# A plain latent attention's first keys and queries in another order, and a down product that waits chunk by chunk

## What the kernel computes

```
q_hk  = (hidden_q @ Wq.T).reshape(b, s, H, K)
q_big = einsum('bshk,hkq->bshq', q_hk, w_kc_q)
kv_rope = kv_c * cos + rotate_half(kv_c) * sin
q_r = einsum('bshq,hqr->bhsr', q_big, W_qr)
k_r = einsum('bld,hdr->bhlr', kv_rope, W_kr)
scores = einsum('bhsr,bhlr->bhsl', q_r, k_r)
attn = softmax(scores);  ctx_c = einsum('bhsl,bld->bhsd', attn, kv_rope)
out  = (ctx_c @ w_kc_kv per head).reshape(...) @ Wo.T
```

```
x = fwht(x * SU_ug) / 64
x = silu(x @ W_gate.T * sg) * (x @ W_up.T * su)      # 1024 wide
x = fwht(x * SU_dp) / 64;   x = x @ W_down.T * (Wscale_dp * 64)
```

## Time and profile before

| | |
|---|---|
| runs | 1613.93, 1619.74, 1620.39 us; median 1619.74 |
| the profiled execution | 1614.18 us, span 1612.3 us |
| busy: PE, weight loads (PEld) | 1512.9 us (94%), 1216.2 us (75%) |
| busy: DVE, ACT, POOL | 893.1, 658.6, 691.6 us (55, 41 and 43%) |
| mean granted clock of TensorE | 0.98 |

### The profile page before, as it was taken

How to read it: one execution, slowest core, us unless ns; L and a number is a source line. 1 busy time by engine, 2 the same in 40 slices (tenths; PEclk the granted TensorE clock), 3 DMA queues, 4 the chain that set the end, 5 groups by cost and what they waited for, 6 DMA issues and landing times. The chain is left out here.

```text
span 1612.3 us, 39418 instructions
## 1 busy us (share of the span) xinstructions
PE 1512.9 (94%) x17044; PEld 1216.2 (75%) x17056; DVE 893.1 (55%) x1623; ACT 658.6 (41%) x955; POOL 691.6 (43%) x506
## 2 busy tenths in 40 slices
PE   6897899999999999888998999999999999898998
PEld 3583688888888877676656888888888779746466
DVE  4950565766666536875546555556565153377212
ACT  3543344454444442652013444444444434244221
POOL 5308364465446200633966644664451026180101
PEclk9998899999999999999998999999999999899999
DMA  8045265654563302314035646535541030152402
GB/s 241 2 106 113 65 146 135 140 120 106 118 149 73 73 7 94 111 60 121 0 69 123 140 110 137 122 91 120 133 91 29 15 108 1 34 217 63 160 24 66
DMA packets 66460, 154.45 MB, mean 96 GB/s; under 512 B 14972, under 2 KB 44220, under 8 KB 65424
## 3 DMA queue, kind: packets, MB, share of 16 engines
q1 hardware_dynamic: 65520, 150.10, 37.2%
q0 software_dynamic: 768, 1.84, 0.4%
HBM read 87.51 MB, written 5.51 MB: 58 GB/s over the span
## 5 line engine op out<-in xcount | busy, mean ns | idle before, releaser
L1726 DVE TENSOR_REDUCE latent_psW<-latent_psW 128x1 f32<-128x500 f32 x642 | 411.0, 682 | 224.1 <-PE latent_psW L1622 223.4
L1705 ACT ACTIVATE latent_w<-latent_psS 125x896 f32<-125x896 f32 x384 | 351.7, 919 | 409.7 <-PE latent_psS L1640 406.3
L1650 PEld LDWEIGHTS latent_psO<-latent_val,latent_w 125*64 125x64 f32 x10752 | 324.2, 138 | 24.9 <-issue 11.5
L1650 PE MATMUL latent_psO<-latent_val,latent_w 125*64 125x65 f32 x10752 | 339.9, 223 | 0.2 <-issue 0.2
L1639 PE MATMUL latent_psS<-latent_qA,latent_kA 128*125 128x448 f32 x768 | 290.4, 378 | 6.1 <-DVE latent_qB L1743 4.3
L1640 PE MATMUL latent_psS<-latent_qB,latent_kB 128*125 128x448 f32 x768 | 282.6, 368 | 0.0
L1622 PE MATMUL latent_psW<-latent_kA,latent_qA 128*128 128x500 f32 x642 | 208.2, 394 | 0.6
L1639 PEld LDWEIGHTS latent_psS<-latent_qA,latent_kA 128*125 128x125 f32 x768 | 143.5, 187 | 33.5 <-DVE latent_qB L1743 4.9
L1640 PEld LDWEIGHTS latent_psS<-latent_qB,latent_kB 128*125 128x125 f32 x768 | 143.6, 187 | 19.9
L1622 PEld LDWEIGHTS latent_psW<-latent_kA,latent_qA 128*128 128x128 f32 x642 | 122.2, 191 | 13.9 <-DVE latent_psW L1726 2.4
L1003 POOL TENSOR_TENSOR latent_rawT<-latent_rawT,latent_ropeT 128x1000 f32<-128x1000 f32 x48 | 110.5, 2329 | 41.2 <-DVE all_xn L267 33.6
(11 more groups left out here) (424 smaller groups left out, 2230.0 us busy)
## 6 DMA issues: line engine op xcount, KB each, us to landing
latent_qA<-latent_qh SPq DMA_DIRECT2D x128, 112.0 KB, 2.5
latent_rawT<-in_ctx_cols SPq DMA_DIRECT2D x32, 375.0 KB, 5.3
latent_rawT<-in_ctx_cols SPq DMA_DIRECT2D x64, 187.5 KB, 5.8
latent_raw<-in_ctx SPq DMA_DIRECT2D x32, 375.0 KB
latent_kA<-latent_high SPq DMA_DIRECT2D x32, 375.0 KB, 3.8
latent_kB<-latent_high SPq DMA_DIRECT2D x32, 375.0 KB, 5.3
latent_kA<-latent_rawT SPq DMA_DIRECT2D x32, 375.0 KB, 6.2
experts_wgu<-in_L_gu SPq DMA_DIRECT2D x8, 1024.0 KB, 16.2
```

What stands on the lines that cost most here:

```text
L1650: last = pe.matmul(sums[r:r + 64, c, :], w[t % ROUND][:, queries_of(c, r):queries_of(c, r) + 64], val[b % 2][:, t, :], start=(t == 0 and c ...
L1705: act.activation(w[t % ROUND][:, :].rearrange("p (h n) -> p h n", h=2), psS[0:KP, t % 2, :, 0:GH], ACT.Exp).then_inc(exp_done, 1)
L1726: dve.tensor_reduce(bank[:, THIRD + j:THIRD + j + 1], bank[:, 0:THIRD], mybir.AxisListType.X, ALU.max).then_inc(max_ready, 1)
```

## The change

**In the plain queries' stage**

- GpSimd takes the first keys' low parts directly behind their rotation, and rotates the value rows only behind the low queries.
- ScalarE rounds the high keys behind the copy of step 0, no longer of step 2.
- SyncE loads the mask here, ahead of all stores; then it stores batch 0's keys, batch 0's queries, and batch 1's keys last. The mask's buffer is placed in this stage for the plain layer alone; the roped layer loads it in the attention as before.
- TensorE starts with the scores for the maxima behind queries' step 11 and no longer 10, and weaves in 4, 4, 4, 4 and 5 in place of 3, 3, 3, 4, 4 and 4.

**In the rotated feed-forward stage** `FIRST_FOLD` goes from 7 to 5, and the wait for all 16 low parts ahead of the down product becomes a wait for each chunk in the first tile, and for all in front of the fifth tile.

```diff
             def _(sp):
                 ...
-                first.store_queries(sp)
+                first.load_mask(sp)
+                first.store_keys(sp, 0)
+                first.store_queries(sp, keys=False)
+                first.store_keys(sp, 1)
             def _(pool):
                 pool.wait_ge(norm.xn_ready, NT)
                 first.rope_keys(pool, 0)
+                first.low_keys(pool, 0)
                 first.fill(pool)
-                first.rope_rows(pool, 0)
-                first.low_keys(pool, 0)
                 first.empty_queries(pool, norm)
                 first.low_queries(pool, q)
+                first.rope_rows(pool, 0)
                 first.rope_keys(pool, 1)
...
-                    if n == 2 * HP - 6:
+                    if n == 2 * HP - 5:
                         pe.wait_ge(f["taken"], HP)
                         pe.wait_ge(first.kA_came[0], 48)
                         pe.wait_ge(first.qA_came[0], 64)
-                    for _ in range(max(0, n - 2 * HP + 7) and (3 if n < 2 * HP - 3 else 4)):
+                    for _ in range(0 if n < 2 * HP - 5 else 4 if n < 2 * HP - 1 else 5):
...
-                    if n == 2:
+                    if n == 0:
                         first.high_keys(act, 0)
...
-                sp.dma_start(mask[:, :, :], ...).then_inc(mask_came, 16)
+                if not n.maxima_made:
+                    n.load_mask(sp)
                 store_queries(1)
...
-        FIRST_FOLD = 2 * NF - 1 - NF
+        FIRST_FOLD = 2 * NF - 3 - NF
...
-                    if n > FIRST_FOLD:
+                    if 0 <= n - FIRST_FOLD - 1 < NF:      # GpSimd and ScalarE
...
-                pe.wait_ge(h_split, 2 * NF)
                 for t in range(NT):
                     ...
                     for k in range(NF):
+                        if t == 0:
+                            pe.wait_ge(h_split, 2 * k + 1)
+                        if t == NT // 2 and k == 0:
+                            pe.wait_ge(h_split, 2 * NF)
```

More of the change, by code:

```diff
@@ L916, in place_queries @@
         if self.layer == 1:
+            self.place_mask(self.a)
+        self.mask_came = self.a.sem("mask_came")
+        if self.layer == 1:
             self.rawT.append(self.a.sb("rawT1", [128, 2, LK]))
@@ L935, in low_queries, with place_mask, load_mask, store_queries @@
                            self.qh[:, :].bitcast(F32).rearrange("p (j s) -> p j s", s=S), ALU.subtract).then_inc(self.ql_ready, 1)
-    def store_queries(self, sp):
+    def place_mask(self, a):
+        self.mask = a.sb("mask", [self.MAX_ROWS, NH * S // 128, 128])
+    def load_mask(self, sp):
+        sp.dma_start(self.mask[:, :, :], self.d["max_mask"].rearrange("p (c n) -> p c n", n=128)).then_inc(self.mask_came, 16)
+    def store_queries(self, sp, keys=True):
         GH = HP * S
-        self.store(sp)
+        if keys:
+            self.store(sp)
         sp.wait_ge(self.qh_ready, 1)
@@ L1508, in latent_attention @@
         w += [a.sb(f"w{u}", [KP, G8]) for u in range(2, ROUND)]
-        mask = a.sb("mask", [MAX_ROWS, QTL, 128])
+        if not n.maxima_made:
+            n.place_mask(a)
+        mask, mask_came = n.mask, n.mask_came
         mx = n.mx
@@ L1526, in latent_attention @@
         max_scores, max_ready, maxima_ready = n.max_scores, n.max_ready, n.maxima_ready
-        names = ("mask_came", "cleared", "max_turned", "row_ready",
+        names = ("cleared", "max_turned", "row_ready",
                  "scores_done", "exp_done", "av_done", "rec_ready", "o_ready", "out_turned", "out_taken")
-        (mask_came, cleared, max_turned, row_ready,
+        (cleared, max_turned, row_ready,
          scores_done, exp_done, av_done, rec_ready, o_ready, out_turned, out_taken) = (a.sem(n) for n in names)
@@ L1556, in load_magnitudes @@
                     sp.dma_start(lanes[m % 2][:, 1:1 + PIECE], d["L1_lanes"][:, m * PIECE:(m + 1) * PIECE]).then_inc(lanes_came[m % 2], 16)
-                sp.dma_start(mask[:, :, :], d["max_mask"].rearrange("p (c n) -> p c n", n=128)).then_inc(mask_came, 16)
+                if not n.maxima_made:
+                    n.load_mask(sp)
                 store_queries(1)
@@ L2400, in _ @@
                         round_hidden(n - 1)
-                    if n > FIRST_FOLD:
+                    if 0 <= n - FIRST_FOLD - 1 < NF:
                         round_weights(n - FIRST_FOLD - 1)
```

## The result

The changed kernel took 1602.65 us (median of 4 runs, 1601.08 to 1603.84), against 1618.82 us of the kernel before (4 runs, 1613.93 to 1620.39). The ratio is 0.9905, with a 95% interval of 0.9881 to 0.9928, and the time is 16.2 us less by the medians. The forecast was 1601 us. By the ratios that is 15, 21 and 19 us.

What follows compares the result with a forecast made beforehand. TensorE, busy 94% of 1612.3 us, bounds the kernel by its idle gaps and lower clock. Terms of 11.5 + 1.5 + 4.7 = 17.7 us give 1596.5 from the profiled run, 1602.0 from the median; forecast 1601 us, range 1594 to 1606.

Steps and rivals of the forecast that it cites:

- Term 1: Plain queries' stage: stores land before TensorE needs them, so the stage ends 11.5 us sooner (9.5 to 12).
- the two pieces: Plain queries' stage: 8.1 us from the earlier start, the rest from the lower clock and the step already done.
- the bound of 4.75 us: Plain queries' stage: if the four stores issue as slowly as before, TensorE waits 1.6 us.
- the rival of the late queries: Plain queries' stage: stores need 1.2 us each, TensorE waits 1.6 us at step 11; 1603.5 us, chance 0.13.
- the rival "slower": Plain queries' stage: VectorE's maxima and GpSimd's work hold each other up; 1628 us at 1.85 us each; chance 0.02.
- Term 2: Attention's start: early mask and perhaps fuller clock, less a new wait for batch 1's queries; 1.5 us (0 to 3).
- the 1.8 us: Attention's start: with the mask already there, the first score starts at 180.95 in place of 182.78.
- the 3.5 us that I had forecast: End of the plain queries' stage: TensorE idles some 3.5 us after its last score, while VectorE finishes five maxima.
- Term 3: Rotated feed-forward: the 3.04 us gap and the lower clock behind it go; 4.7 us (3.0 to 5).
- The rival that only the feed-forward works: Plain queries' stage: keys land as late, so the wait stays; about 5 us gained, 1615 us, chance 0.06.

Runs made afterwards that it cites:

- e5: The changed kernel with GpSimd's old order, value rows ahead of the first low keys; 1608.56 us.
- e1: The kernel before with the feed-forward's edits alone; 1614.6 us, 0.9974 of before.
- e2: The changed kernel without the feed-forward's edits; 1603.34 us, 0.9902 of before.
- e4: The kernel before with SyncE's order alone: batch 0's keys, the queries, then batch 1's keys; 1615.11 us.
- e10: The changed kernel again, with nothing altered; 1595.83 us, 0.987 of before.
- e11: The changed kernel again, with nothing altered; 1598.85 us, 0.9881 of before.
- e6: The changed kernel with the folds back at step 7, the waits by chunk kept; 1603.99 us.
- e7: The changed kernel with one wait for all low parts again, the folds kept at step 5; 1606.63 us.
- e9: The changed kernel with 20 idle products behind the last scores for the maxima and the mask's load back at the attention's start; 1597.01 us, 0.9864 of before.

## Why the prediction was right, step by step

**Term 1, the plain queries' stage: 11.5 us forecast, 12.1 measured.** It came in the two pieces that the working named. The first score stands 17.80 us behind the first queries' product in place of 26.41, 8.6 us sooner (forecast 8.1), and the rest, from there to the attention, is 13.99 us in place of 17.50, 3.5 less (forecast 3.4). The stores' issue took 2.39 us, as the row of the roped stage said, and the bound of 4.75 us didn't come true; the rival of the late queries fell. e5 shows that this hung on the low keys' store being out of the way. The forecast was that the stores land 0.7 us ahead of TensorE (151.7 against 152.4); it was 0.2, since TensorE came 17.80 us behind its first product and not 18.3. Against e1's stage of 44.83 us the gain is 13.0 and not 12.1, so the size hangs by 0.9 us on which profile of the old arrangement is taken. Single steps were off and cancelled:

- GpSimd waited 1.55 us for the high keys, not 2.8. Its rotation ended later than before relative to the queries (at 137.28, 2.3 us behind the first product, against 0.8), and the high keys, rounded as soon as it had ended, came at 138.76. In e2, where the rotation ended 1.0 us behind the first product, GpSimd waited 2.76 us, as forecast, and the stage was as long (31.79).
- The low keys' store took 4.3 us to land and not 3.7. There was room for it.
- GpSimd ended 0.4 us ahead of VectorE, not 1.2: counted from the first queries' product, it was 0.4 us later than forecast (31.1 against 164.8 - 134.07 = 30.7) and VectorE 0.5 sooner (31.46 against 31.9). Its work beside the maxima wasn't stretched: its last keys' steps are 3.65 us, where they were 3.63. In the changed kernel this engine is next in line: with 0.4 us of room, another microsecond of work on it would cost some 0.6, by estimate.
- The maxima took 0.60 us each beside a GpSimd that was never idle: 5.00 of 5.00 us from 155 to 160. The condition of the rival "slower" never came, and so its price wasn't tested.

By the Trainium skill, "SBUF — State Buffer", Who interferes with whom, a `tensor_reduce` on this chip never contends with GpSimd. The trace agrees: nine maxima in the 5.00 us from 155 to 160 with GpSimd busy for all of them, where before eight took 4.86 us with GpSimd idle.

**Term 2, the attention's start: 1.5 us forecast.** The profiled pair shows nothing here (425.53 and 425.47 us for the attention), which is the lower end of my range. Over all profiles it is another picture. The three with the old arrangement (before, e1, e4) have 425.4 us on average, the seven with the new one and no filler (after, e10, e11, e2, e5, e6, e7) 423.7, so 1.7 us less, with single values from 422.4 to 425.5. Most of what differs lies at the start, 13.8 against 12.4 us to the first values: what follows them is 411.0 to 411.9 us in every kernel of the table. Within the new arrangement it is the clock that decides there, not the mask. In after it was low for about 10 us from 166, in e10 and e11 for some 7, in e2 and e7 for 3 to 4, in e5 and with a filler not at all, and the first values came at 14.1, 12.8, 11.7 and 11.2 us.

My working priced the mask at 1.8 - 0.9 = 0.9 us; e9 shows 0. The wait for batch 1's `qA` that I had added, 0.9 us, is there (0.73). What was wrong is the 1.8 us. In e9 the late mask holds the first score up by 3.36 - 2.92 = 0.4 us, and the wait for `qA` is shorter by as much and hides all of it. I had taken the 1.8 from a single profile, in which VectorE waited 3.58 us for the mask; in e9 it waited 2.14, and e1's first score, with the mask late too, stood 1.2 us sooner than before's. So the step failed in its reason, and that its size came out near the mean of seven is luck.

What makes the 1.7 us is open. Set side by side by how long the clock was low at this start, the old arrangement has 13.7 us to the first values (before, 3 us low), 12.9 (e1, 7) and 14.7 (e4, 10), the new one 11.7, 12.8 and 14.1. So something may be left for the new arrangement, 0.1 to 2.0 us, but with one old profile at each length, and 3 us of scatter from the clock, it may as well be chance.

By the Trainium skill, "TensorE: Matmul & The Clock Gate", Part 1, an idle stretch as long as the 3.5 us that I had forecast brings the lower clock, by which term 2 would have been 0.9. The stretch was 2.65 to 2.70 us, and in six of the seven profiles without filler the clock did fall there, in e5 it didn't. The same part says that how much runs at the lower clock varies from run to run; the spread of 11.7 to 14.1 us bears that out.

**Term 3, the rotated feed-forward: 4.7 us forecast, 4.6 measured**, and 83.87 - 79.04 = 4.8 between the means of the three with the old arrangement (before, e2, e4) and the nine with the whole new one. The working held in each step: no gap, the first tile in 3.03 us (forecast 2.9), the first fold 19.95 us behind the stage's start (at 1334.39; forecast 19.7), 5.3 us behind the end of the butterflies (forecast 5). What the prediction didn't say is that both edits are needed, which e6 and e7 show. It named only the low part of chunk 7 as the last input, and priced the moved folds at nothing; with the folds at their old place it is the last folded weights, for which TensorE waits 1.89 us.

**The sum.** 17.7 us were forecast. The changed stages of the profiled pair are 16.8 us shorter, and the terms as the means give them are 12.1 + 1.7 + 4.8 = 18.6 (19.5 with the 13.0 us against e1); the three comparisons are 15 to 21. That 1601 lies only 1.65 us from the measured 1602.65 is luck in part, since the same kernel's median was 1595.83 and 1598.85 us the next times. The rival that only the feed-forward works fell with e2. The sum counts against medians. Had I compared the two profiled spans alone, 10.3 us, I would have found 7 us missing, and they are no effect of the change: before's profile caught three unchanged stages at their shortest, 243.7 us, and after's at nearly their longest, 249.2. Of the two places that I could count from, the profiled 1614.18 us and the median, the forecast lay nearer to the median's, and that was right. The levels of the runs have a likely cause, the clock at the starts of stages. Each timed run has its mean granted clock on record, and in the 16 runs of before that stand beside e1 the time falls with it: the four slowest, 1620.52 to 1620.84 us, had 0.974 or 0.975, the two fastest, 1613.05 and 1613.89, had 0.980 and 0.979 (the correlation over the 16 is -0.76). That the clock makes all of the spread isn't shown: one of 1616.95 us had 0.981.

## What to carry to other kernels

When a wait ends with a small store, look at what stands ahead of it in the queue, and then at who makes the input of that: with one order alone the first score still stands 4.9 us later than with both. A gap of TensorE ahead of a dense stretch costs its length and, where the clock falls, something on top: here 3.04, 2.77 and 1.89 us of gap cost 4.6, 4.6 and 3.65 us of the stage, 1.6 to 1.9 more than their length, so the last 1.9 us of a gap were worth 3.65, and taking a third of it away brought little. Before a difference between two profiles is put down to a change, subtract the stages that the change doesn't touch: here they scattered by 5.6 us, more than the second or the third term was worth.

## What the runs showed of the hardware

- The same instructions at the same place had 1.00 or 0.57 of the clock over their first 4 us in different executions, and whole stages came out at one of a few lengths: 35.1 or 36.8 us for the output, 78.8, 80.0 to 80.2 or 81.8 to 82.7 for the ternary feed-forward.
- With 20 idle products, in 2.39 us, over a stage's end the clock was 1.00 through the attention's start in all four profiles that had them; without them it was so in one of the seven of the same arrangement. What they gave there was not to be seen in the time of the whole.
- After gaps of 1.89, 2.77, 3.01, 3.01 and 3.04 us ahead of the down product (e6, e7, e2, e4, before) the clock fell to 0.50 every time; in the nine profiles without a gap it stayed at 1.00. After the same 2.65 to 2.70 us ahead of the attention it was low for 10, 7, 3 or 0 us.
- Four stores of the same 64 x 448 tiles took 2.39 us to be issued on an empty queue, 3.12 directly behind a store of keys, and 4.75 behind three of them; they landed in 2.1 to 2.3 us on the empty queue, and 2.7 to 3.6 behind the one.
- The same kernel had medians of 1602.65, 1595.83 and 1598.85 us in three comparisons, while before stood at 1618.5 to 1619.1 in all.
